# Two layers on one core: VectorE's loop over image pairs written out, and the end of an image cut into pieces that run in later steps

## The chip, the cores and the metric

The kernel runs on one core of a Trainium2 chip. The metric is the time on the device in microseconds, lower is better. The kernel before takes 31037.8 us (median of three runs, 31033.51 to 31046.34).

## The reference

The input is a batch of 32 images of 96 channels and 56 x 56 pixels, all in float32. Two layers follow each other. Cut to what matters for this change:

```
# layer 0
h = conv7x7_depthwise(x) + conv_b
h = (h - mean_c(h)) * rsqrt(var_c(h) + 1e-5) * ln_g + ln_b      # over the 96 channels
h = gelu(h @ w1 + b1) @ w2 + b2                                   # 96 -> 384 -> 96
x = h * layer_scale + x
# layer 1, its beginning
mean, var = over the pixels of one image and channel
x_act = silu(gamma * (x - mean) / sqrt(var + 1e-5) + beta)
# ... windows of 8 x 8 pixels, projections, a 3 x 3 convolution, four selective scans ...
out = x + alpha * (x_act windows + result of the scans)
```

Layer 0 as the kernel has it ends with two arrays in device memory that layer 1 reads: `act_d`, which is x_act, and `base_d`, which is x + alpha * x_act.

## The kernel before

`layer0` and `layer1` are two blocks, one after the other. In each, every engine runs an instruction stream of its own, and the order in a stream is written out by hand; the streams meet at semaphores alone. The change lies in `layer0`.

An image is cut into NR = 7 strips of 8 rows (RT = 448 pixels on 96 partitions). A *step* is one strip; a *pair* is two images, STEPS = 14 steps, and there are 16 pairs. Two buffers (`par` 0 and 1) hold the two images of a pair: `shifted` (the image three times over, as TensorE's part of the convolution wants it), `image`, `mixed` (the output of the MLP plus the image) and `acted`.

What a step s of pair i does, by engine:

- **TensorE** (L285 to L322): the up projection of strip n into `hid_p` (L296, six matmuls), the centring of strip n+1 (L272), a third of its share of the convolution of strip n+2 (L262), the variance matmul of strip n+1 (L276), which waits for ACT's square, another third of the convolution, the down projection (L306), the last third. It loops over the pairs 0 to 14 and has the last pair written out.
- **ScalarE** (L362): three Gelus (L341), the square (L328), Ln and Exp for the deviation (L334, L336), and the exit from the MLP (`leave_mlp`, L348). Gelu, Ln/Exp and Silu lie in different tables, so a step has two table loads and an image's silu adds one. In step 0 it also ran `finish` for the second image of the pair before, in step 7 for the first image of this pair.
- **VectorE** (L504): 14 of its 26 taps of the convolution of strip n+2 (`conv_below`, L434 and L437), then xn of strip n+1 (`normalise`, L456), which TensorE's next up projection waits for, the other taps, then `add_image` (L464 and the statistics, L469; on an image's last strip also L475 and L476), which waits for ACT's exit from the MLP, and `add_below` (L443, and L449, which writes h_sb for the next centring). In steps 0 and 7 it ran `finish`. Pair 0 and pair 15 are written out, pairs 1 to 14 are a loop on the engine (L521). In the loop the semaphore values depend on a register, so register instructions stand beside the waits.
- **GpSimd** stores `acted` and `mixed` of an image (L229, L230) when the semaphore `based` tells that it is complete.
- **SyncE** loads an image of the next pair when the convolution and `mixed` of the same buffer have used up the one before.

`finish` of an image was a chain over two engines: ACT waits for the image's mean and variance (`mv_done`) and makes the reciprocal deviation (L354, L356); VectorE makes the scale and the shift (L481, L485); ACT runs one silu over the whole image, 96 x 3136 (L358); VectorE waits for it and adds alpha * silu to the whole image (L489). Each engine ran its part in one go and waited in between.

Of the kernel before, what the change touches and what calls it, by code (L numbers as in the profile page):

```python
# [15 lines left out]
RT = ROWS * W  # L16
NR = H // ROWS
STEPS = 2 * NR
HID = 4 * C
HC3 = HID // 128  # L20
TAPS = 7
# [61 lines left out]
def layer0(nc, x, conv_w, conv_b, ln_g, ln_b, w1, b1, w2, b2, layer_scale, gamma, beta, alpha, act_d, base_d):  # L83
    NB = x.shape[0]
    ctx = ExitStack()
    with ctx:
# [12 lines left out]
        mixed = sb("mixed", [C, 2, PIX])  # L99
        acted = sb("acted", [C, 2, PIX])  # L100
# [22 lines left out]
        vec = sb("vec", [C, 8])  # L123
# [37 lines left out]
        acted_done = sem("acted_done")  # L161
        based = sem("based")
# [5 lines left out]
        with nc.Block() as block:  # L168
# [24 lines left out]
            def _(pool):  # L193
# [37 lines left out]

                with pool.Fori(0, NB // 2, 1) as i:
                    for par in range(2):
                        pool.wait_ge(based, i * 2 + par + 1)
                        store(i * 2 + par, par)
                for par in range(2):
                    pool.wait_ge(stored[par], NB // 2 * 32)
# [85 lines left out]
            def _(act):  # L323
# [24 lines left out]
                    nc.scalar.activation(mlp[:], out_p[:, 0:RT], ACT.Identity, scale=vec[:, 4:5],  # L348
                                         bias=lsb[:, 0:1]).then_inc(mlp_done, 1)

                def finish(i, par):
                    b = i * 2 + par
                    act.wait_ge(mv_done, b + 1)
                    nc.scalar.activation(istd[:, 0:1], mv[:, 1:2], ACT.Ln, bias=eps[:, 0:1]).then_inc(ivar_done, 1)  # L354
                    act.wait_ge(ivar_done, b + 1)
                    nc.scalar.activation(istd[:, 1:2], istd[:, 0:1], ACT.Exp, scale=-0.5).then_inc(istd_done, 1)  # L356
                    act.wait_ge(scale_done, b + 1)
                    nc.scalar.activation(acted[:, par, :], mixed[:, par, :], ACT.Silu, scale=scale[:, par, 0:1],  # L358
                                         bias=scale[:, par, 1:2]).then_inc(acted_done, 1)
# [3 lines left out]
                def body(i, first=False, last=False):  # L363
                    for s in range(STEPS):
                        n = i * STEPS + s
                        hidden(n)
                        if not (last and s == STEPS - 1):
                            squares(n + 1)
                            deviation(n + 1)
                        leave_mlp(n)  # L370

                        if s == 0 and not first:
                            finish(i - 1, 1)
                        if s == NR:
                            finish(i, 0)

                squares(0)
                deviation(0)
# [2 lines left out]
                    with act.Fori(1, NB // 2 - 1, 1) as i:  # L381
                        body(i)
                body(NB // 2 - 1, last=True)
                finish(NB // 2 - 1, 1)

            @block.vector
            def _(dve):
# [17 lines left out]
                for k in range(HC3):  # L405
                    last = nc.vector.tensor_tensor(b1g[:, k:k + 1], hid_p[k][:, 0:1], b1_s[:, k:k + 1], ALU.add)  # L406
# [68 lines left out]
                        nc.vector.tensor_copy(scale[:, par, 0:1], vec[:, 5:6])  # L475
                        nc.vector.bn_aggr(mv[:], stats[:]).then_inc(mv_done, 1)  # L476

                def finish(i, par):
                    b = i * 2 + par
                    dve.wait_ge(istd_done, b + 1)  # L480
                    nc.vector.tensor_tensor(scale[:, par, 0:1], scale[:, par, 0:1], istd[:, 1:2],  # L481
                                            ALU.mult).then_inc(chain, 1)
                    dve.wait_ge(chain, b * 2 + 2)

                    nc.vector.scalar_tensor_tensor(scale[:, par, 1:2], mv[:, 0:1], scale[:, par, 0:1], vec[:, 6:7],  # L485
                                                   ALU.mult,
                                                   ALU.subtract, reverse1=True).then_inc(scale_done, 1)
                    dve.wait_ge(acted_done, b + 1)
                    nc.vector.scalar_tensor_tensor(mixed[:, par, :], acted[:, par, :], vec[:, 7:8], mixed[:, par, :],  # L489
                                                   ALU.mult, ALU.add).then_inc(based, 1)  # L490

                every = range(len(dtaps))
# [1 line left out]
                def body(i, first=False, last=False):  # L494
                    for s in range(STEPS):
                        more = s + 2 < STEPS or not last
                        ahead = (i, s + 2) if s + 2 < STEPS else (i + 1, s + 2 - STEPS)
                        if more:
                            conv_below(*ahead, every[:CUT])
                        if not (last and s == STEPS - 1):  # L500
                            normalise(i * STEPS + s + 1)
                        if more:
                            conv_below(*ahead, every[CUT:])
                        if not first and s % NR == 0:  # L504
                            dve.wait_ge(stored[s // NR], i * 32)
                        add_image(i, s // NR, s % NR)
                        if more:
                            add_below(*ahead)
                        if s == 0 and not first:
                            finish(i - 1, 1)  # L510
                        if s == NR:
                            finish(i, 0)

                conv_below(0, 0, every)
                add_below(0, 0)
                conv_below(0, 1, every)
                normalise(0)
                add_below(0, 1)
                body(0, first=True)
                if NB // 2 > 2:  # L520
                    with dve.Fori(1, NB // 2 - 1, 1) as i:  # L521
                        body(i)
                body(NB // 2 - 1, last=True)
                finish(NB // 2 - 1, 1)


ROW_ONE, ROW_B, ROW_C = RK, 16, 32
# [1037 lines left out]
```

## Time and profile before

| what | us |
|---|---|
| median of three runs | 31037.8 |
| span of the profiled execution | 31035.4 |
| TensorE busy | 28615.5 (92%) |
| VectorE busy | 27602.9 (89%) |
| ScalarE busy | 24152.4 (78%) |
| GpSimd busy | 25853.7 (83%) |
| L489, the addition for a whole image, x32 | 111.4, mean 3481 ns |

One execution on the chip, taken by the hardware profiler, is what all views of the profile show. "Busy" is the time in which an engine executes data instructions; register, branch and semaphore instructions do not count. "Idle before, releaser" is the time an engine stood still ahead of an instruction, with the instruction of another engine whose semaphore let it go on; "issue" stands where the profile shows nothing that it waited for. PEclk is the clock that TensorE was granted, as a share of full speed. A "step" of layer 0 is seen in TensorE's timeline by its group of six L296 matmuls. Layer 0 fills about the first tenth of the span, layer 1 the rest.

### The profile page before, as it was taken

Reading aid. Unit: us, or ns where it says so; the run is one execution under the profiler, and the core shown is the slowest. Engines: PE = TensorE matmul, PEld = TensorE weight load, DVE = VectorE, ACT = ScalarE, POOL = GpSimd, SP = SyncE. Lnnn points to the kernel's source line nnn. Section 1 sums busy time; section 2 is a strip of 40 time slices with the busy share of each in tenths; the row PEclk is TensorE's granted clock in tenths of the full one; section 3 lists DMA queues with packets and bytes.
Section 4 is the critical chain, followed back from the end, with each engine's and each line's share of the span. In section 5 each row is a group of like instructions: output and inputs, shape, how many; then the busy total and the mean of one; then the engine's idle time right before and its main releaser. Section 6 shows DMA issues by size and latency. Waiting matters only on the chain.

```text
span 31035.4 us, 986155 instructions
## 1 busy us (share of the span) xinstructions
PE 28615.5 (92%) x399070; PEld 10807.2 (35%) x399070; DVE 27602.9 (89%) x18447; ACT 24152.4 (78%) x37826; POOL 25853.7 (83%) x13288
## 2 busy tenths in 40 slices
PE   8999799999999999999999999999999999999998
PEld 2333233333333333333333333333333333333333
DVE  7888799999999999999999999999999999999998
ACT  4555688888888888888888888888888888888887
POOL 0000599999999999999999999999999999999999
PEclk9999999999999999999999999999999999999999
DMA  3333344444444444444444444444444444444444
GB/s 82 88 84 82 79 103 99 102 98 102 99 101 100 100 100 100 101 100 102 99 102 100 101 99 101 99 103 98 103 98 102 100 102 99 102 98 102 98 102 90
DMA packets 3821867, 3043.32 MB, mean 98 GB/s; under 512 B 2184848, under 2 KB 2987792, under 8 KB 3796944
## 3 DMA queue, kind: packets, MB, share of 16 engines
q1 hardware_dynamic: 3809888, 2910.77, 44.4%
q8 instruction: 3312, 54.26, 0.8%
q0 software_dynamic: 8560, 77.41, 0.7%
q14 instruction: 107, 0.88, 0.0%
HBM read 2325.71 MB, written 449.58 MB: 89 GB/s over the span
## 4 chain that ended last, share of the span: by engine, by line
PE 28%; POOL 20%; issue 18%; ACT 13%; DVE 8%; DMA 1%; POOLq 0%; SPq 0%; ACTq 0%; DVEq 0%
POOL state L942 17%; PE dbu L1032 9%; PE pp L1126 7%; DVE state L1477 5%; ACT state L1256 5%; PE yb L1051 4%; DVE dg L1467 2%; PE pp L1100 2%; POOL dd L949 2%; PE pp L1089 1%; PE pp L1120 1%; ACT sp_w L1333 1%; POOL dd L962 1%; ACT sp_v L1334 1%; PE b_t L1068 1%
## 5 line engine op out<-in xcount | busy, mean ns | idle before, releaser
L942 POOL TENSOR_TENSOR state<-state,cc 128x1024 f32<-128x1024 f32 x9408 | 22044.2, 2375 | 1411.5 <-DVE state L1477 1381.9
L1477 DVE TENSOR_TENSOR_SCAN state<-state,dbu 128x1024 f32<-128x1024 f32 x9408 | 21000.9, 2269 | 2295.8 <-PE dbu L1032 2292.6
L1256 ACT ACTIVATE state<-dl,a_neg 128x512 f32<-128x512 f32 x18816 | 12250.6, 711 | 21.2 <-DMA dl<-dlx 1.4
L1032 PE MATMUL dbu<-dg,du_t 64*32 64x256 f32 x301056 | 10198.2, 383 | 968.5 <-DVE state L1477 895.6
L1032 PEld LDWEIGHTS dbu<-dg,du_t 64*32 64x32 f32 x301056 | 5100.0, 106 | 7276.9 <-issue 6198.1
L1051 PE MATMUL yb<-state,mask 128*32 128x512 f32 x37632 | 5078.5, 612 | 2.2 <-POOL state L942 2.2
L1467 DVE TENSOR_TENSOR dg<-b_t,mask_q 128x1024 f32<-128x1024 f32 x3136 | 3757.7, 1198 | 41.4 <-PE b_t L1068 41.4
L229 POOL DMA_DIRECT2D act_d<-acted x32 | 16.3, 509 | 3218.2 <-DVE mixed L489 2909.2
L1126 PE MATMUL pp<-sp_a,minus 128*128 128x512 f32 x2352 | 1321.4, 644 | 587.4 <-ACT ye L1284 252.1
L1339 ACT ACTIVATE sp_y<-pp 128x512 f32<-128x512 f32 x1176 | 704.2, 599 | 1440.4 <-PE pp L1126 1417.1
L437 DVE SCALAR_TENSOR_TENSOR acc<-image,cw_v,acc 96x432 f32<-96x432 f32 (+2 forms) x2912 | 1687.6, 647 | 0.0
L262 PE MATMUL conv_p<-shifted,cw 128*32 128x424 f32 (+3 forms) x12096 | 1646.1, 542 | 0.4 <-DVE b1g L406 0.4
L949 POOL TENSOR_TENSOR dd<-sp_r,sp_y 128x512 f32<-128x512 f32 x1176 | 1507.9, 1282 | 111.3 <-ACT sp_y L1339 111.3
L1051 PEld LDWEIGHTS yb<-state,mask 128*32 128x32 f32 x37632 | 743.7, 108 | 1962.1 <-issue 1783.5
L1120 PE MATMUL pp<-xd,dt_l 128*128 128x512 f32 x2352 | 1324.4, 645 | 102.9 <-ACT xd L1308 81.5
L1126 PE MATMUL pp<-sp_w,minus 128*128 128x512 f32 x2352 | 1202.8, 593 | 0.0
L1126 PE MATMUL pp<-sp_v,minus 128*128 128x512 f32 x2352 | 1202.5, 593 | 0.0
L1347 ACT ACTIVATE du_t<-pp 128x512 f32<-128x512 f32 x1176 | 683.7, 581 | 541.2 <-PE pp L1133 540.6
L1325 ACT ACTIVATE sp_a<-pp 128x512 f32<-128x512 f32 x1176 | 698.9, 594 | 516.2 <-POOL dd L949 271.3
L1100 PE MATMUL pp<-xs,cw 96*32 96x448 f32 (+1 forms) x7056 | 1009.1, 563 | 12.7 <-DMA xs<-ye 9.1
L1308 ACT ACTIVATE xd<-pp,one_row 64x512 f32<-64x512 f32 x784 | 535.6, 683 | 608.4 <-PE pp L1109 603.4
L964 POOL TENSOR_TENSOR dd<-dd,u 128x512 f32<-128x512 f32 x588 | 902.7, 1535 | 92.7 <-POOL dd L949 62.1
(174 smaller groups left out, 26584.2 us busy)
## 6 DMA issues: line engine op xcount, KB each, us to landing
dl<-dlx SPq DMA_DIRECT2D x4704, 256.0 KB, 4.7
cc<-cd SPq DMA_DIRECT2D x3136, 256.0 KB, 6.2
dlx<-dd SPq DMA_DIRECT2D x1176, 256.0 KB, 2.0
shifted<-in_x SPq DMA_DIRECT2D x384, 392.0 KB, 12.5
xs<-ye SPq DMA_DIRECT2D x1176, 112.0 KB, 2.8
xs<-ye SPq DMA_DIRECT2D x588, 128.0 KB, 2.6
image<-in_x SPq DMA_DIRECT2D x32, 1176.0 KB, 24.5
act_d<-acted POOLq DMA_DIRECT2D x32, 1176.0 KB, 9.1
```

Of the source, the lines that this page charges most:

```text
L262: last = nc.tensor.matmul(dst[:, :, lo:hi], cw[:, cb * PCOLS + w, :], src.rearrange("p (i j) -> p i j", j=W)[:, :, lo + e:hi + e], start=t ...
L437: nc.vector.scalar_tensor_tensor(dst, src, weight, dst, ALU.mult, ALU.add).then_inc(tap_done, 1)
L942: nc.gpsimd.tensor_tensor(its, its, cc[:, h, s, :], ALU.mult).then_inc(hc_done, 1)
L949: nc.gpsimd.tensor_tensor(dd[:, 0, :], sp_r[:], sp_y[:], ALU.add).then_inc(dl_done, 1)
L1032: last = nc.tensor.matmul(dst[:, :, TQ * e:TQ * e + TQ], du_t[its, j, col:col + JC], dg[its, h, 2 * k + s, MG * TQ * g:MG * TQ * g + MG * ...
L1051: last = nc.tensor.matmul(bank[JC * m:JC * m + JC, :].rearrange("p (k q t) -> p k q t", k=2, t=WPX), mask[:], src[:, ::-1, ::-1, ::-1] if ...
L1100: last = nc.tensor.matmul(windows(pp[32 * q:32 * q + 32, :])[:, :, :, a:c], cw[:, 3 * cb + d, :], windows(xs[:, 2 * (cb % 3) + cb // 3, :] ...
L1120: nc.tensor.matmul(pp[:], dt_l[:, f, j, :], xd[:, f, :], start=True, stop=True).then_inc(pp_ready, 1)
L1126: last = nc.tensor.matmul(pp[:], minus[:, i, :], part[:], start=i == 0, stop=i == 2)
L1256: nc.scalar.activation(state[:, slot, :, m * WPX:m * WPX + WPX].rearrange("p (q k) t -> p q k t", k=2), by_place(dl[:, J // 2, 2 * h + J % ...
L1467: nc.vector.tensor_tensor(dg[:, h, blk, :].rearrange("p (n t) -> p n t", t=TQ), b_t[:, col:col + NS].unsqueeze(2).broadcast_to([128, NS, TQ]),
L1477: nc.vector.tensor_tensor_scan(its, its, dbu[p % 2][:], 0.0, ALU.mult, ALU.add).then_inc(scan_done, 1)
```

## The change

1. VectorE's loop over the pairs 1 to 14 is replaced by a Python loop that writes all 16 pairs out. The waits on VectorE then hold constants. TensorE's, ScalarE's, GpSimd's and SyncE's loops stay.
2. `finish` on ScalarE becomes `deviation_of_image`, at the end of steps 0 and 7 as before, and `silu_of_image`, at the end of steps 1 and 8.
3. `finish` on VectorE becomes `scale_of_image`, at the head of steps 1 and 8, and `base_of_image`, the addition in three pieces of 19, 19 and 18 rows of pixels, at the end of steps 2, 3, 4 and 9, 10, 11.
4. `based` is raised three times per image, and GpSimd waits for the third.
5. For the last image all pieces run one after the other behind the last step.

```diff
--- before.py
+++ after.py
@@ -16,6 +16,7 @@
 RT = ROWS * W
 NR = H // ROWS
 STEPS = 2 * NR
+THIRDS = [0, 19, 38, 56]
 HID = 4 * C
 HC3 = HID // 128
 TAPS = 7
@@ -231,7 +232,7 @@
 
                 with pool.Fori(0, NB // 2, 1) as i:
                     for par in range(2):
-                        pool.wait_ge(based, i * 2 + par + 1)
+                        pool.wait_ge(based, i * 6 + par * 3 + 3)
                         store(i * 2 + par, par)
                 for par in range(2):
                     pool.wait_ge(stored[par], NB // 2 * 32)
@@ -348,12 +349,15 @@
                     nc.scalar.activation(mlp[:], out_p[:, 0:RT], ACT.Identity, scale=vec[:, 4:5],
                                          bias=lsb[:, 0:1]).then_inc(mlp_done, 1)
 
-                def finish(i, par):
+                def deviation_of_image(i, par):
                     b = i * 2 + par
                     act.wait_ge(mv_done, b + 1)
                     nc.scalar.activation(istd[:, 0:1], mv[:, 1:2], ACT.Ln, bias=eps[:, 0:1]).then_inc(ivar_done, 1)
                     act.wait_ge(ivar_done, b + 1)
                     nc.scalar.activation(istd[:, 1:2], istd[:, 0:1], ACT.Exp, scale=-0.5).then_inc(istd_done, 1)
+
+                def silu_of_image(i, par):
+                    b = i * 2 + par
                     act.wait_ge(scale_done, b + 1)
                     nc.scalar.activation(acted[:, par, :], mixed[:, par, :], ACT.Silu, scale=scale[:, par, 0:1],
                                          bias=scale[:, par, 1:2]).then_inc(acted_done, 1)
@@ -370,9 +374,13 @@
                         leave_mlp(n)
 
                         if s == 0 and not first:
-                            finish(i - 1, 1)
+                            deviation_of_image(i - 1, 1)
+                        if s == 1 and not first:
+                            silu_of_image(i - 1, 1)
                         if s == NR:
-                            finish(i, 0)
+                            deviation_of_image(i, 0)
+                        if s == NR + 1:
+                            silu_of_image(i, 0)
 
                 squares(0)
                 deviation(0)
@@ -381,7 +389,8 @@
                     with act.Fori(1, NB // 2 - 1, 1) as i:
                         body(i)
                 body(NB // 2 - 1, last=True)
-                finish(NB // 2 - 1, 1)
+                deviation_of_image(NB // 2 - 1, 1)
+                silu_of_image(NB // 2 - 1, 1)
 
             @block.vector
             def _(dve):
@@ -475,7 +484,7 @@
                         nc.vector.tensor_copy(scale[:, par, 0:1], vec[:, 5:6])
                         nc.vector.bn_aggr(mv[:], stats[:]).then_inc(mv_done, 1)
 
-                def finish(i, par):
+                def scale_of_image(i, par):
                     b = i * 2 + par
                     dve.wait_ge(istd_done, b + 1)
                     nc.vector.tensor_tensor(scale[:, par, 0:1], scale[:, par, 0:1], istd[:, 1:2],
@@ -485,8 +494,11 @@
                     nc.vector.scalar_tensor_tensor(scale[:, par, 1:2], mv[:, 0:1], scale[:, par, 0:1], vec[:, 6:7],
                                                    ALU.mult,
                                                    ALU.subtract, reverse1=True).then_inc(scale_done, 1)
-                    dve.wait_ge(acted_done, b + 1)
-                    nc.vector.scalar_tensor_tensor(mixed[:, par, :], acted[:, par, :], vec[:, 7:8], mixed[:, par, :],
+
+                def base_of_image(i, par, part):
+                    its = slice(THIRDS[part] * W, THIRDS[part + 1] * W)
+                    dve.wait_ge(acted_done, i * 2 + par + 1)
+                    nc.vector.scalar_tensor_tensor(mixed[:, par, its], acted[:, par, its], vec[:, 7:8], mixed[:, par, its],
                                                    ALU.mult, ALU.add).then_inc(based, 1)
 
                 every = range(len(dtaps))
@@ -495,6 +507,10 @@
                     for s in range(STEPS):
                         more = s + 2 < STEPS or not last
                         ahead = (i, s + 2) if s + 2 < STEPS else (i + 1, s + 2 - STEPS)
+                        if s == 1 and not first:
+                            scale_of_image(i - 1, 1)
+                        if s == NR + 1:
+                            scale_of_image(i, 0)
                         if more:
                             conv_below(*ahead, every[:CUT])
                         if not (last and s == STEPS - 1):
@@ -506,22 +522,21 @@
                         add_image(i, s // NR, s % NR)
                         if more:
                             add_below(*ahead)
-                        if s == 0 and not first:
-                            finish(i - 1, 1)
-                        if s == NR:
-                            finish(i, 0)
+                        if 2 <= s < 5 and not first:
+                            base_of_image(i - 1, 1, s - 2)
+                        if NR + 2 <= s < NR + 5:
+                            base_of_image(i, 0, s - NR - 2)
 
                 conv_below(0, 0, every)
                 add_below(0, 0)
                 conv_below(0, 1, every)
                 normalise(0)
                 add_below(0, 1)
-                body(0, first=True)
-                if NB // 2 > 2:
-                    with dve.Fori(1, NB // 2 - 1, 1) as i:
-                        body(i)
-                body(NB // 2 - 1, last=True)
-                finish(NB // 2 - 1, 1)
+                for i in range(NB // 2):
+                    body(i, first=i == 0, last=i == NB // 2 - 1)
+                scale_of_image(NB // 2 - 1, 1)
+                for part in range(3):
+                    base_of_image(NB // 2 - 1, 1, part)
 
 
 ROW_ONE, ROW_B, ROW_C = RK, 16, 32
```

## Rows read from the trace of the kernel before

**Rows 1.** Windows: start:end, length, busy us (count) by engine, PEclk, DMA share, GB/s

```profile
89.60:3292.70 3203.10, 3070.73 (x15557) 1003.29 (x15557) 2601.86 (x4662) 1680.15 (x2129) 31.53 (x62) 0.98 0.33 81
1089.30:1292.60 203.30, 194.62 (x981) 63.72 (x981) 164.15 (x295) 105.85 (x134) 2.03 (x4) 0.97 0.34 84
10000.00:10140.20 140.20, 129.52 (x1960) 49.84 (x1956) 127.45 (x72) 114.66 (x183) 131.71 (x68) 1.00 0.48 101
```

**Rows 2.** Timeline of TensorE, regular steps: start us, us, engine line op out<-in xcount

```profile
1138.49 2.52 PE L296 MATMUL hid_p<-xn,w1g 96*128 96x448 f32 x6
...
1165.51 2.52 PE L296 MATMUL hid_p<-xn,w1g 96*128 96x448 f32 x6
```

**Rows 3.** Line L296: durations, first and last start; last two groups in the timeline

```profile
L296 PE MATMUL hid_p<-xn,w1g x1344: 539/539/1112, 89.6 to 3294.7; 96*128 96x448 f32 x192
...
3285.58 2.52 PE L296 MATMUL hid_p<-xn,w1g 96*128 96x448 f32 x6
...
3292.69 2.52 PE L296 MATMUL hid_p<-xn,w1g 96*128 96x448 f32 x6
```

**Rows 4.** List of waits of TensorE, layer 0: us in total, times, longest us

```profile
PE var_p L276 <- ACT sq L328: 78.2, 31, 3.5
...
PE hid_p L296 <- DVE xn L456: 26.1, 21, 3.5
PE hid_p L296 <- issue: 20.1, 14, 1.8
PE cen_p L272 <- DVE h_sb L449: 8.9, 18, 0.8
```

**Rows 5.** Timeline of TensorE behind a turn of the loops, [idle before <-releaser]

```profile
1089.30 2.52 PE L296 MATMUL hid_p<-xn,w1g 96*128 96x448 f32 x6 [1.22 <-issue]
...
1105.52 4.18 PE L296 MATMUL hid_p<-xn,w1g 96*128 96x448 f32 x6 [2.63 <-DVE xn L456]
...
1115.29 0.99 PE L276 MATMUL var_p<-sq,mean 96*96 96x448 f32 x2 [2.48 <-ACT sq L328]
```

**Rows 6.** Timeline of VectorE at the same place

```profile
1097.10 0.81 DVE L434 TENSOR_SCALAR acc<-image,cw_v 96x448 f32<-96x448 f32 x2 [7.63 <-issue]
...
1111.86 3.48 DVE L489 SCALAR_TENSOR_TENSOR mixed<-acted,vec,mixed 96x3136 f32<-96x3136 f32 x1 [3.07 <-ACT acted L358]
```

**Rows 7.** Windows of the same place, columns as in rows 1

```profile
1083.98:1100.20 16.22, 15.01 (x75) 4.97 (x73) 6.48 (x15) 6.94 (x9) 0.00 (x0) 1.00 0.76 163
1100.20:1119.65 19.45, 14.34 (x62) 4.53 (x64) 16.27 (x27) 11.28 (x13) 1.01 (x2) 0.83 0.92 212
```

**Rows 8.** Timeline of ScalarE, the end of a pair's first image

```profile
1609.55 0.72 ACT L348 ACTIVATE mlp<-out_p,lsb,vec 96x448 f32<-96x448 f32 x1 [3.52 <-PE out_p L306]
...
1610.71 1.28 ACT L358 ACT_TABLE_LOAD   x1
1613.23 3.00 ACT L358 ACTIVATE acted<-mixed,scale 96x3136 f32<-96x3136 f32 x1 [1.24 <-DVE scale L485]
```

**Rows 9.** Timeline of TensorE, the same place

```profile
1619.70 0.99 PE L276 MATMUL var_p<-sq,mean 96*96 96x448 f32 x2 [2.35 <-ACT sq L328]
```

**Rows 10.** Timeline of ScalarE, a regular step

```profile
1136.29 0.72 ACT L348 ACTIVATE mlp<-out_p,lsb,vec 96x448 f32<-96x448 f32 x1 [3.52 <-PE out_p L306]
1137.03 1.28 ACT L341 ACT_TABLE_LOAD   x1
```

**Rows 11.** Timeline of VectorE, a regular step

```profile
1150.56 0.62 DVE L464 TENSOR_TENSOR mixed<-mlp,image 96x448 f32<-96x448 f32 x1 [2.03 <-ACT mlp L348]
```

**Rows 12.** List of waits of VectorE, first pair, its longest

```profile
DVE mixed L464 <- ACT mlp L348: 26.9, 13, 3.2
```

**Rows 13.** Lines of VectorE: us busy, mean ns | idle before

```profile
L443 DVE SCALAR_TENSOR_TENSOR acc<-acc,vec 96x448 f32<-96x448 f32 x224 | 147.2, 657 | 0.0
...
L489 DVE SCALAR_TENSOR_TENSOR mixed<-acted,vec,mixed 96x3136 f32<-96x3136 f32 x32 | 111.4, 3481 | 99.1 <-ACT acted L358 99.1
```

**Rows 14.** Tile mixed, the store of base_d: from issue to landing

```profile
DMA to landing us min/median/max: 10.0/12.3/13.4
```

## What the change should do to the time

> **What bounds the kernel now.** The change touches layer 0 only, so I first cut the span by stretch with the windows view. Layer 0's steps run from the first matmul of L296 at 89.6 to that of the last step at 3292.69 [rows 3], 3203.1 us; everything else is layer 1, some launch work and the end of layer 0. In that stretch TensorE is busy 3070.7 us, VectorE 2601.9 and ScalarE 1680.2 [rows 1]. So TensorE leads, with 132.4 us idle and a mean granted clock of 0.98 [rows 1]. The question is who makes it idle, and who makes its clock fall.
>
> For that I take a step with nothing in its way. From one L296 to the second one after it are 1165.51 - 1138.49 = 27.02 us [rows 2], 13.51 us a step, without an idle entry between: this is TensorE's own pace at the full level of 2.4 GHz. The last interval, in which no convolution runs any more, is 3292.69 - 3285.58 = 7.11 us [rows 3]. The 16 pairs have 224 steps (1344 matmuls of L296, six to a step [rows 3]), so 223 intervals. At the pace of TensorE alone they would take 222 x 13.51 + 7.11 = 3006.3 us. They take 3203.1. **The excess is 196.8 us, and only that can be won.** It has two parts: the 132.4 us of idle time and 64.4 us more, which a clock of 0.98 over 3203 us explains (0.02 x 3203 = 64).
>
> The list of TensorE's waits names the idle time [rows 4]: 78.2 us in 31 waits of the variance matmul for ACT's square, 26.1 us for VectorE's xn, 8.9 us for VectorE's h_sb, and 20.1 us in 14 waits that the profile puts to "issue". The timeline shows each in its place [rows 5]: 1.22 us where TensorE's own loop turns (14 turns, the 20.1 us), 2.63 us one step later for xn, 2.48 us in the step after for the square. The 14 are not touched: TensorE's loop stays.
>
> Why is xn late? VectorE stands still for 7.63 us before the first tap of its loop body, released by nothing [rows 6]; that is its loop's turn, once in each of the 13 passes back. Then, from the scale on, it stands 3.07 us for the silu and takes 3.48 us for the addition of a whole image [rows 6], once per image. Why is the square late? ACT, after leaving the MLP at 1609.55, does two tiny operations, loads silu's table at 1610.71, waits 1.24 us for VectorE's scale and runs the silu of an image, 3.00 us from 1613.23 [rows 8]; the hidden layer of the next step and its square queue behind that, and TensorE waits 2.35 us [rows 9].
>
> **The clock.** In the 16 us about TensorE's 1.22 us idle time the granted clock is 1.00; in the step that holds the 2.63 and 2.48 us ones it is 0.83 [rows 7], a stretch at 1.2 GHz each time (six matmuls of L296 take 4.18 us there [rows 5] against 2.52 in a regular step [rows 2]). So the long stalls are paid a second time, the short one not. The Trainium skill ("TensorE: Matmul & The Clock Gate", Part 1) has it that "the ramp penalty is <1% of a typical kernel span"; by that one would leave the clock out of the sum and come to the second case below, while these rows put 64 us on the clock beside 91 us of removable waits.
>
> **The change part by part.**
> (a) VectorE's loop written out. The 13 turns, each some 7.6 us as the one read, go. In the first pair, written out already, VectorE's list of waits has no "issue" entry at all; the longest is the ordinary wait for the MLP, 26.9 us in 13 [rows 12]. So nothing replaces them by this profile. The register instructions of the waits go too; they hid beside other work, so I count them at nothing.
> (b) The scale. Its two tiny operations now come at the head of step 1 (and 8), a step after ACT made the deviation, so neither engine waits there: ACT's 1.24 us [rows 8] and VectorE's stay in the queue are gone.
> (c) The silu comes one step later, behind that step's exit from the MLP. In a regular step the next table load begins 1137.03 - 1136.29 = 0.74 us after the exit's start [rows 10]. So silu's table can load at 1609.55 + 0.74 = 1610.29 and the silu starts at 1610.29 + 1.28 + 0.03 = 1611.60 instead of 1613.23: 1.63 us earlier against the same step of TensorE. The table and the silu itself remain in front of the hidden layer, so the stall is not gone but shrinks from 2.35 [rows 9] to 0.7 us. All 31 silus that lie beside TensorE's steps keep it: 31 x 0.7 = 21.7 us. Bounds: 0 (if the square has room that I miss) and 2.35 us (if nothing is won), 0 to 73 us.
> (d) The addition in thirds. A whole image is 3481 ns for 3136 columns, the same kind of operation 657 ns for 448 [rows 13]; a line through both gives 1.05 ns a column and 0.19 us fixed, so a third of 1064 columns is 1.3 us (bounds: 1.16, a third of 3.48, and 1.56, 657 ns scaled by columns). Three cost 3.85 us instead of 3.48, but each stands at the end of steps 2 to 4 (9 to 11). What hides it: VectorE idles 2.03 us before L464 in such a step [rows 11]; 1.3 fits in it, as does the scale in step 1. Nobody waits behind it: the silu ended a step earlier. Uncovered it would cost at most 1.3 us x 3 x 31 = 121 us.
> (e) The store. POOL now waits for the third third, so both stores leave three steps later; POOL queues nothing else. The second of them landed 10.0 to 13.4 us after issue [rows 14]. VectorE needs them by the same slot's next first row, three steps (40 us) on. They also leave the time in which the next image is loaded. No cost.
> (f) The end of layer 0, where no step covers anything: three thirds instead of one, + 0.4 us.
>
> **The sum.** Excess 196.8; what stays is 20.1 (TensorE's turns) and 21.7 (silu), and 0.4 is added: 196.8 - 20.1 - 21.7 - 0.4 = 154.6 us off. This supposes that the clock stays up, since the idle times left (1.22 to 1.8 and 0.7 us) are of the size that left it at 1.00 [rows 7]. The profiled span is 31035.4 us, the median 31037.8, 2.4 more. 31035.4 - 154.6 + 2.4 = **30883 us** (-0.50%). What is late next in layer 0 is nobody: 93 to 99% of each step is TensorE's own pace.
>
> **The rivals.**
> 1. *The clock does not come back.* The 31 short stalls follow each other with a turn, and stretches at 1.2 GHz remain. Then only the waits are won: 26.1 + 8.9 + 78.2 - 21.7 - 0.4 = 91.1 us, 30947. For it: the profile has no stall of 0.7 us with its clock. Against: the longer 1.22 us left the clock at 1.00 [rows 7]. A silu that is less early than in (c) lands between the two.
> 2. *The written-out VectorE code runs dry somewhere in each pair*, as the loop's turn did. Then xn's 26.1, h_sb's 8.9 and about half of the 64.4 us remain, 67 us: 30883 + 67 = 30950; twice per pair, 31017, which is no change. Against: the first pair [rows 12].
> 3. *The stall of a turn appears in layer 1.* Its loops move, since VectorE's code before them grows by 13 pairs. Layer 1's VectorE loop makes 194 passes of 140.2 us [rows 1]; if each began with 7.63 us as layer 0's did [rows 6], that is 1480 us, less what its 12.7 us of idle time (140.20 - 127.45 [rows 1]) take up, from which point it decides; with half taken up, 31037.8 - 155 + 740 = 31620, slower. Against: it has 72 busy instructions a turn, where layer 0's has 295 [rows 1], and turns free now. The Trainium skill ("Runtime: NRT & Kernel Launch", Instruction fetch mechanics) says that an engine holds two blocks of 256 instructions and that a taken branch outside them waits for a fetch; by it the place of a middling loop decides, which speaks for a small chance of this on ACT or VectorE. No run shows it yet.
> 4. *It doesn't do what it says*: the thirds or the later silu stand in the way and eat the gain (the 121 us of (d)): 30883 + 121 = 31004, no change.
>
> **How the numbers follow.** Forecast 0.66 (30862 with no silu stall left, 30905 with 1.4 us of it); rival 1 and what lies between, 0.14; rival 2, 0.09, of which 0.02 as no change; rival 3, 0.05; rival 4, 0.06. The range reaches from 30862 to 30950: forecast, rival 1 and the single stall of rival 2. A measurement of this kernel tells 0.2% (62 us) from no change: faster below 30975.7 is 0.66 + 0.14 + 0.07 = 0.87; within, 0.02 + 0.06 = 0.08; slower 0.05.
>
> **What would show it.** In the profile after: no "issue" wait before L434 on VectorE; L296 13.5 us apart in all steps but those of the 14 turns and 31 silus; a variance wait of 0.7 us in step 2 and 9 for ACT's square, about 22 us in all; no wait for xn; a mean clock near 1.00 in layer 0; layer 0's steps over in some 3050 us; L464 still with some 0.7 us of idle time in steps 3 and 10. Wrong would be: a clock still at 0.98, VectorE idle without a releaser, or a layer 1 whose length moved by more than 10 us.

## The result, and the profile after

The changed kernel takes 30897.8 us (median of four runs, 30884.7 to 30907.7), the kernel before 31041.5 us over the four runs that now stand beside it: 143.6 us or 0.46% less, ratio 0.9954 with a 95% interval of 0.9940 to 0.9968. The forecast was 30883, range 30862 to 30950.

The profiled execution is 30893.6 us long, 141.8 less than before. First the same two views as [rows 1] and [rows 3]: the window over layer 0's steps (from the first matmul of the up projection, now L297, to that of the last step) and the line itself.

```profile
89.60:3150.90 3061.30, 3016.64 (x15557) 995.38 (x15556) 2601.67 (x4724) 1680.49 (x2130) 31.50 (x62) 1.00 0.35 84
```

```profile
L297 PE MATMUL hid_p<-xn,w1g x1344: 539/539/954, 89.3 to 3152.5; 96*128 96x448 f32 x192
```

The steps took 3203.1 us and now take 3061.3: 141.8 us less, all of what the span lost. What lies outside them, layer 1 above all, takes 27832.3 us in both profiled executions. That the two agree to 0.1 us is chance: a second profiled run of the changed kernel (e5_after_again below) has 27818.7. TensorE's idle time went from 132.4 to 3061.3 - 3016.6 = 44.7 us, and its clock is 1.00 where it was 0.98. The waits of TensorE (as [rows 4]) and all the waits of VectorE within layer 0's steps (as [rows 12]):

```profile
PE var_p L277 <- ACT sq L329: 22.8, 32, 0.7
PE hid_p L297 <- issue: 21.9, 14, 1.9
```

```profile
DVE mixed L473 <- ACT mlp L349: 351.5, 191, 3.2
DVE mixed L473 <- issue: 70.4, 30, 3.1
DVE xn L465 <- ACT rstd L337: 9.1, 7, 3.5
```

xn (26.1 us before) and h_sb (8.9) are down to a single wait of 0.2 us within the steps, the square went from 78.2 to 22.8 and its longest from 3.5 to 0.7; what the profile calls "issue" is the turn of TensorE's own loop, as before. VectorE has no entry before its first tap any more; the "issue" entries at L473 end with ACT's exit from the MLP as their neighbours do.

The same turn of the loops as in [rows 5] and [rows 6], TensorE, VectorE and ScalarE in turn:

```profile
1068.16 2.52 PE L297 MATMUL hid_p<-xn,w1g 96*128 96x448 f32 x6
...
1081.68 2.52 PE L297 MATMUL hid_p<-xn,w1g 96*128 96x448 f32 x6
...
1087.99 0.99 PE L277 MATMUL var_p<-sq,mean 96*96 96x448 f32 x2 [0.71 <-ACT sq L329]
```

```profile
1069.21 0.15 DVE L490 TENSOR_TENSOR scale<-scale,istd 96x1 f32<-96x1 f32 x1
1069.39 0.21 DVE L494 SCALAR_TENSOR_TENSOR scale<-mv,scale,vec 96x1 f32<-96x1 f32 x1
1069.53 0.81 DVE L443 TENSOR_SCALAR acc<-image,cw_v 96x448 f32<-96x448 f32 x2
...
1096.97 1.31 DVE L501 SCALAR_TENSOR_TENSOR mixed<-acted,vec,mixed 96x1064 f32<-96x1064 f32 x1
...
1108.03 0.62 DVE L473 TENSOR_TENSOR mixed<-mlp,image 96x448 f32<-96x448 f32 x1 [0.89 <-ACT mlp L349]
```

```profile
1079.48 0.72 ACT L349 ACTIVATE mlp<-out_p,lsb,vec 96x448 f32<-96x448 f32 x1 [3.52 <-PE out_p L307]
1080.22 1.28 ACT L362 ACT_TABLE_LOAD   x1
1081.52 3.00 ACT L362 ACTIVATE acted<-mixed,scale 96x3136 f32<-96x3136 f32 x1
```

From step 1 (1068.16) to step 2 (1081.68) are 13.52 us, where the kernel before took 19.45 [rows 7]. VectorE goes from the scale straight to its taps, a third of the addition takes 1.31 us and leaves 0.89 us of idle time before the next L473. ACT's silu starts 1.30 us after its table load, with no wait for the scale, and TensorE still waits 0.71 us for the square behind it.

### The profile page after: what moved, and what is told of

Same layout as the page of the kernel before. It is cut to its first block, busy times and chain, and to the rows that moved or that the text cites. A ratio compares the mean times of both kernels' runs of the same rounds, so it can differ in the third digit from the quotient of the medians.

```text
span 30893.6 us, 983292 instructions
## 1 busy us (share of the span) xinstructions
PE 28582.9 (93%) x399070; PEld 10799.3 (35%) x399070; DVE 27605.5 (89%) x18511; ACT 24151.6 (78%) x37826; POOL 25854.5 (84%) x13288
## 4 chain that ended last, share of the span: by engine, by line
PE 29%; POOL 20%; issue 18%; ACT 13%; DVE 8%; DMA 1%; POOLq 0%; SPq 0%; ACTq 0%; DVEq 0%
POOL state L957 17%; PE dbu L1047 10%; PE pp L1141 7%; DVE state L1492 5%; ACT state L1271 5%; PE yb L1066 4%; PE pp L1115 2%; DVE dg L1482 2%; POOL dd L964 2%; PE pp L1104 1%; PE pp L1135 1%; ACT sp_w L1348 1%; ACT sp_v L1349 1%; POOL dd L977 1%; PE b_t L1083 1%
## 5 line engine op out<-in xcount | busy, mean ns | idle before, releaser
L446 DVE SCALAR_TENSOR_TENSOR acc<-image,cw_v,acc 96x432 f32<-96x432 f32 (+2 forms) x2912 | 1687.6, 647 | 0.0
```

The costliest lines, as they stand in the source:

```text
L446: nc.vector.scalar_tensor_tensor(dst, src, weight, dst, ALU.mult, ALU.add).then_inc(tap_done, 1)
```

## The experiments

The kernels of a group (e1 to e4, e5 to e8, e9 to e12) ran on one chip, with the kernel before beside them; the chips differ by up to 24 us, so kernels are compared by their ratio to the kernel before on their own chip, and by the length of layer 0's steps in their profiles. What lies outside those steps (span less steps) scattered by 35 us between profiled runs of kernels that don't differ there (27813.9 us in e3_whole_addition, 27848.9 in e8_both), so a difference of some 10 us between two medians says little, and the steps say more. They come from one profiled run of each kernel: the changed kernel's two have 3061.3 and 3056.9. "At 1.2 GHz" is what the clock's record in the trace has within layer 0's steps; a microsecond at 1.2 GHz costs half a microsecond. e10 and e11 were run once, for their profiles. The code cuts show the main lines; the same edit for the pair's first image (steps from NR on), semaphore counts and the pieces behind the last step are left out.

| kernel | median us | before on that chip | ratio (95% interval) | layer 0's steps us | stretches at 1.2 GHz: number, us |
|---|---|---|---|---|---|
| before | 31041.5 | - | - | 3203.1 | 27, 116.0 |
| changed | 30897.8 | 31041.5 | 0.9954 (0.9940 to 0.9968) | 3061.3 | 3, 13.7 |
| e1_loop_kept | 30908.6 | 31017.6 | 0.9964 (0.9950 to 0.9978) | 3092.0 | 5, 30.7 |
| e2_written_only | 30969.2 | 31017.6 | 0.9984 (0.9975 to 0.9993) | 3152.1 | 21, 81.9 |
| e3_whole_addition | 30872.0 | 31017.6 | 0.9953 (0.9940 to 0.9967) | 3056.5 | 2, 6.8 |
| e4_silu_early | 30968.8 | 31017.6 | 0.9984 (0.9975 to 0.9993) | 3142.1 | 21, 78.5 |
| e5_after_again | 30888.8 | 31037.0 | 0.9954 (0.9940 to 0.9967) | 3056.9 | 2, 6.8 |
| e6_tensor_written | 30866.7 | 31037.0 | 0.9947 (0.9933 to 0.9960) | 3031.4 | 0 |
| e7_silu_halves | 30893.2 | 31037.0 | 0.9954 (0.9940 to 0.9968) | 3057.4 | 8, 34.1 |
| e8_both | 30846.9 | 31037.0 | 0.9939 (0.9925 to 0.9953) | 3007.8 | 0 |
| e9_halves_one_piece | 30878.6 | 31033.1 | 0.9949 (0.9935 to 0.9962) | 3034.5 | 3, 10.2 |
| e10_act_two_pairs (one run) | 30901.1 | 31033.1 | - | 3054.0 | 1, 3.4 |
| e11_act_three_pairs (one run) | 30874.9 | 31033.1 | - | 3052.6 | 0 |
| e12_longer_stall | 30895.7 | 31033.1 | 0.9956 (0.9942 to 0.9969) | 3066.4 | 0 |

### One part at a time

**VectorE's loop put back, the rest of the change kept:**

```diff
-                for i in range(NB // 2):
-                    body(i, first=i == 0, last=i == NB // 2 - 1)
+                body(0, first=True)
+                if NB // 2 > 2:
+                    with dve.Fori(1, NB // 2 - 1, 1) as i:
+                        body(i)
+                body(NB // 2 - 1, last=True)
```

> The changed kernel with VectorE's loop over pairs 1 to 14 put back; the late silu and the thirds stay. My theory: the gain has two parts that add. The 13 turns of VectorE's loop each make xn late and the clock falls behind it; by the step times of the kernel before that is 2.0 us in step 0 and 2.0 us in step 1, 4 x 13 = 52 us, so this kernel takes about 30950 us, and its profile shows some 13 idle times of 7 to 8 us before the first tap and about 26 us of waits for xn. Rival: once the silu chain no longer follows on the late step, VectorE catches up by itself and the turns cost almost nothing: 30898 to 30915. Rival: the loop was the main cause: 31000 or more.

Measured: steps of 3092.0 us, 31 to 35 more than the changed kernel's two profiles (3061.3 and 3056.9), and a ratio of 0.9964 against 0.9954. VectorE's waits, then TensorE's:

```profile
DVE acc L443 <- issue: 85.0, 13, 8.3
```

```profile
PE var_p L277 <- ACT sq L329: 22.6, 32, 0.7
PE hid_p L297 <- issue: 21.6, 14, 1.9
PE hid_p L297 <- DVE xn L465: 15.3, 11, 3.3
...
PE cen_p L273 <- DVE h_sb L458: 5.4, 10, 1.0
```

The 13 idle times are as long as before (85.0 us), but TensorE waits 20.7 us for them instead of 35.0, and the clock costs some 10 us more (30.7 us at 1.2 GHz instead of 6.8 to 13.7, half of the difference). The direction is my theory's, the size (52 us) is not: a late VectorE is cheap when nothing of the silu follows in the next step. Both rivals are out: "almost nothing" by the steps and by the medians on this chip (30908.6 against 30872.0 for e3_whole_addition below, whose steps are the changed kernel's), "the main cause" (31000 or more) by far.

**Only the loop written out**, `finish` as before:

```diff
-                body(0, first=True)
-                if NB // 2 > 2:
-                    with dve.Fori(1, NB // 2 - 1, 1) as i:
-                        body(i)
-                body(NB // 2 - 1, last=True)
+                for i in range(NB // 2):
+                    body(i, first=i == 0, last=i == NB // 2 - 1)
```

> The kernel before with VectorE's loop written out and nothing else: the scale, the silu and the addition of an image stay together at the end of steps 0 and 7. My theory: the silu part remains in all 31 images, 3.9 us each against 0.8 in the changed kernel, so 31 x 3.1 = 96 us more than the changed kernel, about 30994 us, with 2.4 us waits for ACT's square and the clock falling behind them. Rival, not additive: written out code alone gives most of the gain since xn's lateness started the clock's falls: 30930 or less.

Measured: 3152.1 us of steps, 91 to 95 more than the changed kernel, as expected, and 51.0 less than before. The waits of TensorE:

```profile
PE var_p L276 <- ACT sq L328: 73.7, 32, 2.4
...
PE hid_p L296 <- issue: 18.3, 14, 1.7
PE cen_p L272 <- DVE h_sb L449: 5.7, 11, 0.8
PE hid_p L296 <- DVE xn L456: 3.5, 11, 0.3
```

The loop alone brings 51 us, the late end of an image alone (e1 against before) 111; together they bring 142 to 146, not 162. The parts overlap by some 18 us. The intervals between TensorE's groups show where: in steps 0 to 2 of a pair, just behind the turn, writing the loop out takes 56 us off while the silu is early (before against e2) and 31 once it is late (e1 against the changed kernel).

**The addition in one piece** at the end of steps 2 and 9:

```diff
-THIRDS = [0, 19, 38, 56]
+THIRDS = [0, 56]
-                        if 2 <= s < 5 and not first:
+                        if s == 2 and not first:
```

> The changed kernel with the addition of an image in one piece of 3.5 us at the end of steps 2 and 9 instead of thirds. My theory: VectorE has 2.0 us of idle time per step and 1.3 us more between h_sb and the centring that reads it, so 0.2 us per image reach TensorE: 6 us in all, 30904 us, not to be told from the changed kernel. Rival: the piece makes xn and h_sb late, TensorE waits 1.5 to 2 us per image and the clock falls as in the kernel before: 30950 to 30960; then the thirds carry a part of the gain.

Measured: ratio 0.9953, steps of 3056.5 us, the same as the changed kernel. VectorE has used up its idle time (L473 follows L446 without a gap) and h_sb is written in time:

```profile
1092.25 3.47 DVE L501 SCALAR_TENSOR_TENSOR mixed<-acted,vec,mixed 96x3136 f32<-96x3136 f32 x1
...
1104.50 0.61 DVE L473 TENSOR_TENSOR mixed<-mlp,image 96x448 f32<-96x448 f32 x1
```

So the cut into thirds carries nothing. What the addition's move to a step in which VectorE does not wait for the silu is worth is the difference between e2, which lacks it, and e4 below, which has it, with the silu early in both.

**The silu back in step 0**, VectorE not waiting for it:

```diff
                         if s == 0 and not first:
                             deviation_of_image(i - 1, 1)
-                        if s == 1 and not first:
                             silu_of_image(i - 1, 1)
```

with `scale_of_image` at the end of steps 0 and 7 on VectorE.

> The changed kernel with the scale and the silu back in steps 0 and 7 as in the kernel before; VectorE stays written out and does not wait for the silu, the thirds stay in steps 2 to 4. ACT waits 1.24 us for the scale again. My theory: the square is late by 2.3 to 2.4 us again in 31 images instead of 0.7, which is 31 x 1.65 = 51 us, and the clock falls behind some of them, 0 to 1.7 us each: 30950 to 31000, with xn never late. Rival: the late silu is worth nothing and what counted was that VectorE doesn't wait for it: 30900.

Measured: 3142.1 us of steps, 81 to 85 more than the changed kernel, ratio 0.9984. TensorE's one wait of any size is the square's; xn was late once, by 0.2 us:

```profile
PE var_p L277 <- ACT sq L329: 73.6, 32, 2.4
```

73.6 - 22.8 = 51 us are the longer waits. The rest, 30 to 34 us, is the clock: 21 stretches at 1.2 GHz instead of 2 or 3. The place of the silu on ScalarE, with the scale that it waits for, is the largest single part of the change. That VectorE no longer waits for the silu is worth 10 us of the steps (e2's 3152.1 against 3142.1 here) and nothing in the medians (30969.2 against 30968.8).

### What is left, and a better kernel

The changed kernel once more, as a neighbour for the next three:

> The changed kernel itself on this chip, so that the next three have it beside them. Theory: ratio to the kernel before 0.995, as first measured, some 142 us less than the kernel before. Rival: the gain depends on the chip or on luck of the clock's falls; then the ratio lies outside 0.994 to 0.997.

The same ratio, 0.9954, on this chip; steps of 3056.9 us.

**TensorE's loop written out too:**

```diff
-                with pe.Fori(0, NB // 2 - 1, 1) as i:
-                    body(i)
+                for i in range(NB // 2 - 1):
+                    body(i)
```

> The changed kernel with TensorE's loop over pairs 0 to 14 written out too. Theory: the 14 turns of TensorE's loop (interval 15.16 us instead of 13.52) go, 23 us, and with them the rare falls of the clock behind them, 0 to 7 us: 23 to 30 us less than the changed kernel. Rival: the longer TensorE program runs dry somewhere or moves layer 1's long loop to a worse place: no gain or slower.

Measured: 22.1 us less than the changed kernel beside it (30888.8 to 30866.7), steps 25.5 us shorter, as expected, no stretch at 1.2 GHz. TensorE's list keeps the square (22.6 us) and has no "issue" entry.

**The silu in halves:**

```diff
-                        if s == 1 and not first:
-                            silu_of_image(i - 1, 1)
+                        if 1 <= s < 3 and not first:
+                            silu_of_image(i - 1, 1, s - 1)
```

> The changed kernel with the silu of an image in two halves of 1568 columns, at the end of steps 1 and 2 (8 and 9), and the thirds one step later. Each half has its own table load. Theory: a half of 1.6 us leaves the square 0.6 us ahead of the variance matmul, so the 31 waits of 0.7 us go (31 x 0.78 = 24 us less than the changed kernel). Rival: the second table load makes the stall appear twice, at 0.1 to 0.7 us each: no gain, or up to 20 us slower.

Measured: no gain, 0.9954. Yet the square's waits are gone. Their place was taken by a wait that I had not named, TensorE's own turn; so the rival's number came, by another mechanism than the rival's. One of the long turns, and from issue to landing the store of `base_d` (tile mixed) that was issued 10 us ahead of it:

```profile
664.17 4.02 PE L297 MATMUL hid_p<-xn,w1g 96*128 96x448 f32 x6 [3.32 <-issue]
```

```profile
DMA to landing us min/median/max: 12.8/12.8/12.8
```

The thirds had moved on to steps 10 to 12, so the stores started just ahead of the turn at the end of step 13. All 14 turns together are 32.3 us instead of 20 to 22, and 8 stretches at 1.2 GHz follow. The trace has a comparison within itself: in six turns the store landed 0.8 to 2.7 us after TensorE had stopped, and these six took 3.1 to 3.5 us; in the other eight it had landed by then, and they took 1.3 to 1.9 us.

**Both together:**

> TensorE's loop written out and the silu in halves together. Theory: 47 to 54 us less than the changed kernel, every interval of layer 0 at 13.52 us and TensorE's granted clock at 1.00 through it; ratio to the kernel before about 0.9938. Rival: the two don't add, since another wait comes up behind them.

Measured: 30846.9 us, 41.9 less than the changed kernel beside it and 190.1 less than the kernel before; the steps are 49.1 us shorter, within the 47 to 54 expected. The window over nearly all its steps:

```profile
89.60:3097.00 3007.40, 3006.72 (x15556) 993.75 (x15556) 2599.72 (x4723) 1721.58 (x2191) 30.41 (x60) 1.00 0.35 85
```

TensorE is busy 3006.7 of 3007.4 us; the steps (3007.8 us) are at TensorE's own pace, 3006.3 by the prediction. This is the best kernel of the study.

**Halves with the addition in one piece** at step 3 (10), so that the stores are over before the turn (the edit against e7_silu_halves):

```diff
-THIRDS = [0, 19, 38, 56]
+THIRDS = [0, 56]
-                        if 3 <= s < 6 and not first:
+                        if s == 3 and not first:
```

> The silu in halves as in e7_silu_halves, and the addition of an image in one piece at the end of step 3 (10), so that the stores leave two steps earlier; TensorE's loop stays. In e7_silu_halves the 31 waits for the square went, but TensorE's idle time where its loop turns grew from 20 to 32 us and the clock fell 8 times; in its trace the second store of an image was still being written when the turn came. Theory: that store slows the fetch at the turn; now it is over before, the turns are back at 20 to 22 us in all, and the kernel takes 20 to 24 us less than the changed kernel, ratio to the kernel before 0.9947. Rival: the halves themselves lengthen the turn, and the kernel takes as long as the changed one, 0.9954.

Measured: steps of 3034.5 us, 22.9 less than e7_silu_halves and 22 to 27 less than the changed kernel's; the turns are back:

```profile
PE hid_p L297 <- issue: 20.5, 14, 1.8
```

The base_d store now lands some 25 us ahead of the turn, and no turn is longer than 1.8 us. So the halves themselves don't lengthen the turn; the store in front of it does, as far as this kernel, whose addition is also in one piece, and the comparison within e7 can tell. The ratio, 0.9949, lies between the two expectations; its steps follow the theory.

### The turn of a loop, and the clock

**ScalarE's loop over two and over three pairs a pass:**

```diff
-                if NB // 2 > 2:
-                    with act.Fori(1, NB // 2 - 1, 1) as i:
-                        body(i)
+                with act.Fori(0, 7, 1) as i:
+                    body(i * 2 + 1)
+                    body(i * 2 + 2)
```

With three pairs the loop makes 4 passes, and pairs 13 and 14 are written out behind it.

> The changed kernel with ScalarE's loop over two pairs a pass, 7 passes, so the body doubles from 209 records of the trace to some 417. VectorE's body of 521 records stood 7.6 us at each turn, ScalarE's of 209 not at all. Theory: what counts is whether the start of the body is still held when the loop turns; 417 is between the two and tells on which side the bound lies: below 0.5 us if a body of that length is still held, 6 to 8 us of ScalarE idle time at 6 turns if not. I expect it still held. Rival: the cost of a turn is VectorE's own, and neither this nor the next shows any on ScalarE.

> The same with three pairs a pass, 4 passes, some 625 records of the trace in the body, more than VectorE's 521. Theory: ScalarE now stands 6 to 8 us at each of its 3 turns, TensorE waits for Gelu or the square behind it. Rival, the cost is VectorE's own: no idle time at the turns.

ScalarE's waits in layer 0, first with two pairs, then with three (the changed kernel has no such entry):

```profile
ACT L342 <- issue: 12.3, 6, 2.1
```

```profile
ACT L342 <- issue: 6.1, 3, 2.2
```

Two pairs make a body of 416 records, and it already stands 2.0 to 2.1 us at each of its 6 turns; three pairs (623) the same at each of 3. I had expected the first to be free, and it is not; ScalarE's body of 276 in layer 1 is (0.26 us from the branch to the next record). So a standstill at a turn is not VectorE's own, but it is 2.1 us here against VectorE's 7, not the 6 to 8 expected. VectorE's turn falls into the loading of the next image: at 1089.47 to 1097.10 in the kernel before, the DMA engines were busy throughout (share 1.01, 217 GB/s). ScalarE's comes as these loads start: 0.32, 62 GB/s at 663.10 to 665.10 in e10. That this makes the difference is likely from e7 and e9, but it was not tried. TensorE did not feel ScalarE's turns: its wait for the square stayed at 22.9 and 22.6 us.

**A longer stall:** one more operation of ScalarE ahead of each silu (its own semaphore wait left out here):

```diff
                     act.wait_ge(scale_done, b + 1)
+                    nc.scalar.activation(spare[:], mixed[:, par, 0:RT], ACT.Silu).then_inc(spare_done, 1)
```

> The changed kernel with one more ScalarE operation of some 0.6 us (a silu of 448 columns into a spare tile) ahead of each image's silu; nothing reads it. TensorE's 31 waits for the square become 1.25 us instead of 0.7. Theory: 31 x 0.55 = 17 us for the waits, and since idle times of 0.7 us never made the clock fall, those of 2.4 us did in 21 to 24 of 31 and those of 1.2 to 1.9 us at TensorE's turns in 2 or 3 of 14, the clock falls behind a few of them, 0 to 8 times 1.7 us: 17 to 31 us more than the changed kernel. Rival: the clock falls behind nearly all, 70 us more.

```profile
PE var_p L279 <- ACT sq L331: 37.2, 32, 1.2
```

Measured: 14.4 us more of waits and not one stretch at 1.2 GHz in the steps. The steps are 5 to 10 us longer than the changed kernel's, less than the 17 to 31 expected: the waits add 14.4, and the 6.8 to 13.7 us at 1.2 GHz of the changed kernel did not come. Waits for the square of 0.7 us (changed kernel) and 1.2 us left the clock alone every time; those of 2.4 us in e2 and e4 brought it down 21 and 20 times in 31. TensorE's own turns fill the space between, 168 of them in the twelve profiled runs that keep its loop: the clock fell behind none of the 100 below 1.5 us, behind 17 of the 62 of 1.5 to 2.1 us, and behind all six of 3.1 us and more. The length alone does not decide in the middle: in the changed kernel it fell behind turns of 1.63, 1.65 and 1.80 us and not behind those of 1.91 and 1.94.

## Why the prediction was right

The direction, the place and the mechanism were right; of the sum of 154.6 us, 141.8 came in the profile and 143.6 in the medians.

- *The excess over TensorE's own pace* (196.8 us) as the whole of what can be won: shown by e8_both, whose steps take 3007.8 us against 3006.3. Of its two parts the clock's was put at 64.4 us; the clock's record has 116.0 us at 1.2 GHz, which cost 58. The other 6 belong to the stalls, which lengthen an interval by somewhat more than their idle time.
- *(a) the turns of VectorE's loop go and nothing replaces them*: right. No "issue" wait stands before the taps in 16 pairs of written out code; rival 2 is out. The part is worth 31 to 35 us with the silu moved (e1) and 51 with it in its old place (e2).
- *(b), (c) the scale and the late silu*: right, 0.7 us expected, 0.71 measured, 22.8 us in all. I had not seen that this is the largest part (e4).
- *(d) the thirds fit in VectorE's idle time*: 1.31 us measured for 1.3, right but of no account: one piece does as well (e3).
- *(e), (f), the store and the end*: the stores leave 49 us later (the first at 255.2 us, before at 206.4), nearer four steps than the three of (e). They landed in 9.8 to 10.1 us, without a collision. "No cost" held only because they land 13.5 us before TensorE's turn; e7 shows what one step more costs, 10 to 11 us of turns and the clock's falls behind them. The prediction did not see this. The 0.4 us of (f) can't be told in the scatter outside the steps.
- *The clock comes back*: nearly. It fell 3 times for 13.7 us, behind three of TensorE's turns (1.63, 1.65 and 1.80 us), which costs half, 6.8 us. This is rival 1 on a small scale, and the premise was too thin: that 1.22 to 1.8 us leave the clock up was read from one turn of 1.22 us, while the trace of before has a fall right behind its longest turn, 1.83 us at 1901 us.
- *The 12.8 us that are missing*: 6.8 from these stretches; 2.9 from the turns, whose interval is longer by 1.64 us each where the wait list gave 1.44; and 2.5 from the silus (24.2 for 21.7), whose interval is longer by 0.78 where the stall is 0.70. That leaves 0.6 open. The term that was sized too small is "what stays": it counted idle time, where the interval between two groups is what is paid, and nothing for the clock. For the turns this explains 1.0 of the 2.9, since the kernel before's intervals at them add up to 21.1 us; the rest is that they were longer in this run (21.9 us in the list, 18.3 to 21.9 in the kernels with the same TensorE loop and no store beside it).
- *Rival 3, a turn in layer 1*: not seen. The 193 turns of VectorE's loop in layer 1 have their next record 0.22 to 0.25 us after the branch before the change and 0.24 to 0.27 us after it. What lies outside the steps stayed within its scatter (27832.3 us before, 27832.3 and 27818.7 after).
- *Luck*: the forecast of 30883 lies 15 us from the median, while what lies outside the steps moves by 13.6 us between two profiled runs of this very kernel. How well the sum did is told by the steps, 141.8 us for the 155.0 that it takes off there, not by the medians.

## What to carry to other kernels

Find the step in which the leading engine never waits and multiply it: that gives the pace no edit around it can beat, and here it foretold the steps of the best kernel to 1.5 us. Price an edit by the intervals between the leading engine's groups, not by the wait list, since some stalls are paid again in the clock. When a long operation of a second engine must go somewhere, move its preparation a step ahead and let nobody wait for it; and look at what else starts when it ends, as the stores did in front of TensorE's turn.

## What the runs showed of the hardware

- Turning a loop whose body is long cost the engine a standstill: 5.4 to 8.6 us on VectorE with 521 to 525 records of the trace in the body (before, e1), 2.0 to 2.2 us on ScalarE with 416 and 623 (e10, e11), 1.2 to 2.1 us on TensorE with 1041 and 980 weight loads besides; written out, VectorE and TensorE had none (e6, e8). Bodies of 167 (VectorE, layer 1), 209 and 276 records (ScalarE) turned within 0.3 us. The Trainium skill ("Runtime: NRT & Kernel Launch", Instruction fetch mechanics) has two blocks of 256 instructions held (2048 instructions on TensorE) and a fetch for a branch out of what is held; 416 is less than the two blocks, and TensorE's 2021 with the weight loads less than 2048, and neither was free. That ScalarE's body lies across three blocks would explain the first, but was not tried.
- With a store still in flight when it began, TensorE's turn took 3.1 to 3.5 us (six turns of e7), with the store landed 1.3 to 1.9 us (the other eight), with no store near 1.2 to 1.8 us (e9).
- TensorE's clock: after waits of 0.7 and 1.2 us 0 falls in 31 each, after 2.4 us 20 and 21 in 31; behind turns of 1.5 to 2.1 us 17 in 62. A fall lasted 3.4 us, 6.8 in some cases and 10.2 once, and cost half of that. The Trainium skill's "<1% of a typical kernel span" ("TensorE: Matmul & The Clock Gate", Part 1) holds for this span (the mean granted clock over the kernel before is 0.991), but the 58 us in layer 0's steps were 1.8% of these steps and three tenths of what was to be won there.
